# Cross attention and a routed FFN on one core: probabilities turned by transposing DMAs, attention products one body later

## What is computed

```python
q = x @ Wq + lora(x, q);  k = ctx[:, :73] @ Wk + lora(k);  v = ctx[:, :73] @ Wv + lora(v)
out = attention(q, k, v) + attention(q, ctx[:, 73:] @ Wk_ipa, ctx[:, 73:] @ Wv_ipa)
x = x + out @ Wo + bo + lora(out, o)              # x was normalised first
h = layernorm(x);  gate = h @ gate_w              # 8 experts, the best two with weights
x = x + sum over the two experts of  w * (act(h @ w1[e]) @ w2[e])
```

## Time and profile before

| | us |
|---|---|
| median of 3 runs (715.86 to 717.43) | 716.49 |
| the profiled execution | 715.26 |
| span of its profile | 713.5 |
| PE busy (90% of the span) | 639.0 |
| VectorE busy (73%) | 519.7 |
| POOL busy (68%) | 483.3 |
| ACT busy (63%) | 446.3 |

### The profile page before, as it was taken

One profiled execution on the slowest core, in us unless ns is written; L12 is line 12 of the kernel. 1 busy time (PEld: TensorE's weight loads), 2 busy tenths in 40 slices (PEclk: granted clock), 3 DMA queues, 4 the chain that ended last, 5 costly groups with the idle time before them and its releaser, 6 DMA issues. The chain is left out here.

```text
span 713.5 us, 22010 instructions
## 1 busy us (share of the span) xinstructions
PE 639.0 (90%) x7612; PEld 528.3 (74%) x7613; DVE 519.7 (73%) x1226; ACT 446.3 (63%) x768; POOL 483.3 (68%) x577
## 2 busy tenths in 40 slices
PE   6627799999999999999999999979999999999871
PEld 2215587788788888788788778757888888888751
DVE  3964679988988998898898898986577644445431
ACT  1436787778778778778778877854464454454330
POOL 3024645878878877977877887875677676556744
PEclk9999899999999999999999999999999999999997
DMA  8921111112111121111211211203769989655630
GB/s 263 322 79 21 32 34 52 48 45 68 47 55 57 47 62 50 59 53 48 75 36 48 80 32 48 78 16 77 119 124 136 133 119 139 92 82 87 86 48 6
DMA packets 87259, 55.31 MB, mean 78 GB/s; under 512 B 60784, under 2 KB 81520, under 8 KB 87216
## 3 DMA queue, kind: packets, MB, share of 16 engines
q1 hardware_dynamic: 73840, 37.41, 22.2%
q0 software_dynamic: 13376, 17.33, 13.4%
HBM read 20.27 MB, written 24.85 MB: 63 GB/s over the span
## 5 line engine op out<-in xcount | busy, mean ns | idle before, releaser
L527 POOL DMA_INDIRECT out_x<-pt_s,token_of x71 | 113.0, 1592 | 23.4 <-issue 21.4
L782 DVE TENSOR_TENSOR wq_s<-wk_s,wq_s 128x512 f16<-128x512 f32 (+1 forms) x78 | 51.5, 664 | 78.6 <-ACT wq_s L603 78.5
L598 ACT ACTIVATE wk_s<-ps 128x512 f32<-128x512 f32 (+1 forms) x78 | 43.5, 557 | 102.9 <-PE ps L1600 99.0
L1600 PE MATMUL ps<-ffnw,wq_s 128*128 x852 | 100.1, 273 | 6.3 <-DVE wq_s L782 4.8
L1600 PE MATMUL ps<-q_s,ffnw 128*128 128x256 f16 (+1 forms) x936 | 103.3, 264 | 2.1 <-issue 1.6
L959 POOL TENSOR_TENSOR prob<-prob,mx 128x1168 f32<-128x1168 f32 x64 | 77.6, 1233 | 37.6 <-DVE mx L1401 37.5
L1600 PEld LDWEIGHTS ps<-q_s,ffnw 128*128 x936 | 86.0, 98 | 15.2 <-issue 4.6
L1600 PEld LDWEIGHTS ps<-ffnw,wq_s 128*128 128x128 f16 x852 | 81.7, 98 | 19.8 <-issue 9.8
L1600 PE MATMUL ps<-wo_s,ot_s 128*128 128x256 f16 x768 | 89.4, 273 | 2.8 <-DVE ot_s L1338 2.8
L1600 PE MATMUL ps<-xt_s,wq_s 128*128 128x256 f16 x768 | 89.9, 279 | 1.9 <-DVE xt_s L1338 1.9
L1600 PEld LDWEIGHTS ps<-xt_s,wq_s 128*128 128x128 f16 x768 | 76.5, 100 | 13.0 <-issue 1.9
(11 more groups left out here) (232 smaller groups left out, 1176.0 us busy)
## 6 DMA issues: line engine op xcount, KB each, us to landing
wstage<-in_ffn_w SPq DMA_DIRECT2D x16, 512.0 KB, 3.6
x_sb<-in_x SPq DMA_DIRECT2D x4, 1024.0 KB, 10.8
out_x<-x_sb SPq DMA_DIRECT2D x16, 256.0 KB, 2.2
rows_dram<-wstage SPq DMA_DIRECT2D x8, 264.0 KB
out_x<-pt_s,token_of POOLq DMA_INDIRECT x71
pt_s<-in_wq SPq DMA_DIRECT2D x2, 512.0 KB, 4.4
pt_s<-in_wo SPq DMA_DIRECT2D x2, 512.0 KB, 8.4
rows_dram<-row_words,slot_i POOLq DMA_INDIRECT x64, 2.5
```

Of the source, the lines that this page charges most:

```text
L527: pool.indirect_dma_start(out_rows, bass.IndirectOffsetOnAxis(ap=token_of[:, j % UNROLL, c:c + 1], axis=0), y_sb[:, j % UNROLL, c, :], Non ...
L598: act.activation(h32[:, half, 0:2 * n], h_ps(t, j, half)[:, 0:2 * n], ACT.Silu, scale=1 / WSCALE).then_inc(silu_done, 1)
L782: dve.tensor_tensor(hs[:, j % 2, 1, 2 * half:2 * half + 2, 0:n], h32[:, half, 0:2 * n].rearrange("p (f n) -> p f n", f=2), hs[:, j % 2, 0, ...
L1600: last = pe.matmul(o, lhs(a, n), rhs(c, n), start=(i == 0), stop=(i == len(steps) - 1))
```

## The change

1. Scores of both token tiles stay in PSUM, in banks 0 to 2 and 3 to 5. ACT's copies are gone. VectorE takes the maxima from PSUM and subtracts them into `prob` (`shift`, now on VectorE, in four pieces each). Queries, keys and transposes of x use banks 0 to 3, so PE's `queries` wait for the shifts.
2. POOL's `shift` is gone. After `normalise`, ACT writes the high parts token-major into a new tile `p_hl` (`p_high`), POOL the low parts (`p_low`), and SP turns `p_hl` into `pt_s` by four transposing DMAs of 512 KB per body (`columns_p`). PE's transposes of probabilities and their copies remain in the last body alone. The sums are scaled by a new operation, 128x32.
3. Attention products of a body run in the next (`attend_all(b - 1)`); projection, norm, router and routing are one body later too, so three bodies are unrolled, and the last holds more.
4. x and the FFN weights share memory (`both`): weights of 12 to 15 wait until x of the first 8 batches has been stored. `place` lies in PSUM.

```diff
+        both = sb("both", [P, OWN * 2 * FW + TILES * DM * 2], F16)
+        p_hl = sb("p_hl", [P, TPB, 2, HEADS, P], F16)
-        place = sb("place", [P, TPB, EXPERTS], F32)
...
-            return ps[:, (6, 7, 4, 0)[k], :]
+        def queries_bank(b, k):
+            return ps[:, ((6, 7, 4, 0) if only(b, 0) else (0, 1, 2, 3))[k], :]
         def keys_bank(k, b):
+            return ps[:, ((5, 1) if only(b, 0) else (3, 0))[k], :]
+        def scores_bank(t, half, m):
             bank, n = scores_place(half, m)
+            return ps[:, 3 * t + bank, n * CTX:(n + 1) * CTX]
+        def x_bank(b):
+            return ps[:, 4 if only(b, 0) else 7 if only(b, 1) else 0, :]
...
+            def columns_p(t):
+                for part in (0, 1):
+                    sp.dma_start_transpose(pt_s[:, part, :, t * P:t * P + P],
+                                           p_hl[:, t, part].rearrange("p h n -> p (h n)")).then_inc(pt_in[t], 16)
...
                 if not first:
+                    load_fw(b + 1)
+                sp.wait_ge(p_lo, 2 * b + 1)
+                sp.wait_ge(v_mm, b + 1)
+                context_rest(ctx_v, b + 1, ctx_v_in)
+                columns_p(0)
+                if first:
+                    sp.wait_ge(p_lo, 2)
+                    load_fw(1)
+                else:
+                    sp.wait_ge(p_lo, 2 * b + 2)
+                    load_vipa(b)
+                columns_p(1)
...
-            def shift(b, t):
-                pool.wait_ge(mx_done, 2 * b + t + 1)
...
+            def p_low(b, t):
+                pool.wait_ge(p_hi, 2 * b + t + 1)
+                v = prob[:, t, :].rearrange("p (h j) -> p h j", j=CTX)
+                pool.tensor_tensor(p_hl[:, t, 1, :, 0:CTX], v, p_hl[:, t, 0, :, 0:CTX], ALU.subtract).then_inc(p_lo, 1)
...
-            def copy_scores(b, t):
...
+            def p_high(b, t):
+                act.wait_ge(p_ready, 2 * b + t + 1)
+                if not only(b, 0):
+                    act.wait_ge(pt_in[t], 32 * b)
+                act.activation(p_hl[:, t, 0, :, 0:CTX], prob[:, t, :].rearrange("p (h j) -> p h j", j=CTX), ACT.Copy
+                               ).then_inc(p_hi, 1)
...
-            def maxima(b, t):
-                dve.wait_ge(s_copied, 2 * b + t + 1)
+            def shift(b, t):
+                dve.wait_ge(s_mm, 2 * b + t + 1)
...
+                for sc, m, _ in pieces:
+                    for w, ks in ((0, slice(0, ORG)), (1, slice(ORG, CTX))):
+                        last = dve.tensor_reduce(m[:, w], sc[..., ks], AX, ALU.max)
                 last.then_inc(mx_done, 1)
+                dve.wait_ge(mx_done, 2 * b + t + 1)
+                if not only(b, 0):
+                    dve.wait_ge(p_lo, 2 * b + t - 1)
...
+                        last = dve.tensor_tensor(p[..., ks], part, m[:, w].unsqueeze(len(part.shape) - 1).to_broadcast(
+                            list(part.shape)), ALU.subtract)
+                last.then_inc(shifted, 1)
...
+                dve.tensor_scalar(sm[:, t], sm[:, t], 1 / PSCALE, None, ALU.mult).then_inc(sum_done, 1)
...
+            def attend_all(b):
+                for t in range(TPB):
+                    pe.wait_ge(pt_in[t], 32 * b + 32)
...
+                for k in range(4):
+                    if k == 2 and not only(b, 0):
+                        pe.wait_ge(x1_done, b)
+                    if k == 3 and not (isinstance(b, int) and b < 2):
+                        pe.wait_ge(slots, b)
+                    attend(b, k)
...
+                scores(b, 1)
...
+                if normed:
+                    project(b - 2, 1)
+                if routed:
+                    rank(b - 3)
+                pe.wait_ge(xt_split, b + 2)
+                pe.wait_ge(shifted, 2 * b + 1)
+                for k in range(3):
+                    queries(b + 1, k)
+                pe.wait_ge(shifted, 2 * b + 2)
+                queries(b + 1, 3)
+                if not first:
+                    attend_all(b - 1)
...
+                pe.wait_ge(q_split, 4 * b + 8)
+                if x_left:
+                    pe.wait_ge(xt_split, b + 3)
+                new_keys(b + 1)
+                if normed:
+                    pe.wait_ge(ot_split, 4 * b - 3)
+                    transpose_2(b - 2)
                 if not first:
                     project(b - 1, 0)
+                if normed:
+                    router(b - 2)
```

More of the change, by code:

```diff
@@ L288, in build @@
         acc_in = sem("acc_in")
+        acc_old = sem("acc_old")
+        p_hi = sem("p_hi")
+        p_lo = sem("p_lo")
+        pt_in = [sem(f"pt_in{t}") for t in range(TPB)]
         pad_in = sem("pad_in")
@@ L1054, in _ @@
             pool.wait_ge(misc_in, 32)
-            body(0)
-            body(1)
-            with pool.Fori(2, BATCH - 1) as b:
+            for b in range(3):
+                body(b)
+            with pool.Fori(3, BATCH - 1) as b:
                 body(b)
@@ L1499, in _, with body @@
             full_tiles, early_table, late_tables = tile_tables(dve)
[L1501 to L1502 removed]
+            def body(b, x_left):
+                first, normed = only(b, 0), not (isinstance(b, int) and b < 2)
+                routed = not (isinstance(b, int) and b < 3)
                 if routed:
[L1504 to L1522 removed]
+                    chain = pick_experts(b - 3)
+                shift(b, 0)
+                if first:
+                    xt(1)
+                shift(b, 1)
+                q(b + 1, 0)
+                q(b + 1, 1)
+                sums(b, 0)
+                if normed:
+                    attended(b - 2)
+                    statistics(b - 2)
+                if routed:
+                    place_rows(b - 3, chain)
+                q(b + 1, 2)
+                q(b + 1, 3)
+                sums(b, 1)
+                if not first:
+                    for k in range(4):
+                        ot(b - 1, k)
+                if x_left:
+                    xt(b + 2)
@@ L1842, in body @@
[L1842 to L1850 removed]
+                for k, free in ((5, 3), (6, 2), (7, 1)):
+                    pe.wait_ge(pt_split, free)
+                    transpose_probs(b, k)
@@ L1851, in body @@
                 pe.wait_ge(vipa_in, 16 * b + 16)
-                if first:
-                    pe.wait_ge(w_split_p, 3)
+                pe.wait_ge(pt_split, 8)
                 for k in range(4):
-                    pe.wait_ge(pt_split, 8 * b + 5 + k)
-                    if k == 1 and not first and not last:
-                        pe.wait_ge(slots, b)
-                        router(b - 1)
                     attend(b, k)
-            body(0, True, False)
-            body(1, False, False)
@@ L1863, in _ @@
-            with pe.Fori(2, BATCH - 1) as b:
-                body(b, False, False)
-            body(BATCH - 1, False, True)
+            for b in range(3):
+                body(b, True)
+            with pe.Fori(3, BATCH - 2) as b:
+                body(b, True)
+            body(BATCH - 2, False)
+            last_body(BATCH - 1)
             transpose_2(BATCH - 2)
```

470 lines of the change are left out of this document (239 added, 231 removed).

## The result

The changed kernel takes 752.46 us (median of 4 runs, 747.9 to 754.79) against 716.96 for the kernel before beside it: 1.0482 times as long, 95% interval 1.0438 to 1.0527. The forecast was 732, slower, with a range of 702 to 768. The side and the range held, but the loss is 35 us where 15 was forecast. The profiled execution after took 754.79 us, with a span of 753.0.

What follows compares the result with a forecast made beforehand. PE was busiest (25.25 of 26.19 us per body); afterwards VectorE and keys in series would bind at 26.2. 715.26 + 1.4 (head) + 11 x 0.0 - 3.2 (body 14) + 17 (tail) = 730.5, forecast 732 at the median; range 702 to 768.

Steps and rivals of the forecast that it cites:

- The path on VectorE: Loop body: VectorE's operations in program order from the end of the first scores to xt, 18.9 us.
- The scaling of the sums: New VectorE operation of 128x32, twice per body: 0.2 us each, up to 1.8 in the range beside POOL.
- PE's clock full in the loop: Sign expected in the profile after: PE's granted clock stays full (2.4 GHz) through the loop bodies.
- the likeliest case: Loop bodies bound by VectorE and keys in series, 26.2 us each; kernel slower, 722 to 741 us; chance 0.43.
- a rival of 0.12: PE's clock falls in the gap ahead of the keys: 1.5 to 3.4 us per body, 747 to 768; chance 0.12.
- the picks' stall: Head of VectorE's body: picks wait behind POOL's last low part, 0 to 1.65 us, taken as 0.6.
- the head: The three unrolled bodies 0 to 2: +1.4 us in all, range -3 to +6.
- the weights of the next body wait for the low parts; + 2: Body 0 in the head: the next body's FFN weights wait for the low parts; + 2 us.
- The transposing DMAs: SP issues four per body, taken as 2.5 us each; last lands 8.6 us into the next body, at no cost.
- the third rival: Transposing DMAs late: from 3.3 us per issue they hold the attention products; 750 to 775 us; chance 0.15.
- Body 14 and the tail: Body 14 gains 3.2 us; from last scores to first FFN product takes 52 against 34.8, +17 (8 to 22).
- the forecast's next link: Tail: heads of 15 stand behind the norm in ACT's queue, 4.5 us, ahead of VectorE's tables.

Runs made afterwards that it cites:

- The two runs that take the DMAs' wait away: Changed kernel with only the high halves turned by DMA, 744.94 us; changed kernel with all transposes kept but started earlier and body 0's weights loaded first, 742.71 us.
- the last run: Changed kernel with keys, transposes, load and tail changes together, plus eight idle products ahead of the attention products: 707.79 us, 0.9825 of the kernel before.
- both gaps filled: Changed kernel plus idle PE products, ten ahead of the keys and eight ahead of the attention products: 735.39 us, 1.0251 of the kernel before.
- the run with one gap filled: Changed kernel plus ten idle PE products ahead of the keys' wait for xt, bodies 2 to 14: 745.93 us, 1.0420 of the kernel before.
- the run with the load first: Changed kernel with body 0's load of FFN weights for body 1 issued ahead of the transposing DMAs: 745.26 us, 1.0415 of the kernel before.
- the run on the keys: Changed kernel with the keys' second half in bank 5, waiting for the heads' second low part, not xt: 741.18 us, 1.0345 of the kernel before.
- the run on the tail: Changed kernel with the norm of batch 14 ahead of the routing and scatters of 13 in the last body: 747.86 us, 1.0457 of the kernel before.

## Why the prediction was right and wrong

**Right: the mechanism.** The work taken from PE is gone and buys nothing, because the keys wait for xt at the end of VectorE's queue. The path on VectorE was put at 18.9 from the end of the scores and took 18.60 from the first maxima. The two runs that take the DMAs' wait away leave the body at 27.2, and the run that takes xt out of the keys' way has bodies of 24.0 among its eleven.

**Right: VectorE's terms.** The shift was put at 3.3 per token tile and takes 1.63 + 1.63; the low parts on POOL were put at 2.43 and take 2.45. The scaling of the sums was put at 0.2 with 1.8 as the end of its range: it takes 0.18 (POOL idle) and 0.31 to 0.44 in the loop, 1.27 in one body of it, and 1.23 and 1.33 in the last body, where POOL works beside it. That the range of this term comes back in the versions with a shorter body, up to 2.12 us, is what makes some of their bodies long (the last run).

```profile
488.06 1.23 DVE L1489 TENSOR_SCALAR sm<-sm 128x32 f32<-128x32 f32 x1
...
493.32 1.33 DVE L1489 TENSOR_SCALAR sm<-sm 128x32 f32<-128x32 f32 x1
```

The Trainium skill, page "SBUF — State Buffer", section "Who interferes with whom", lists this kind of operation among those that may contend with POOL; these rows, 0.18 against 1.33 for one shape, agree with it.

**Wrong: the body, by one choice.** The step that failed is "PE's clock full in the loop", with which the likeliest case was summed; the loss of the clock after the gap stood as a rival of 0.12, at 1.5 to 3.4 us per body and 747 to 768 us. That rival is what happened, at 1.83 per body or a little more, and its range holds the 752.46. The forecast had weighed one pair of rows, a wait of 3.37 with the clock at half and one of 3.40 with it full, as even evidence. But those two stand in the head, and the path itself said that the gap would come back in every body. What the runs showed in place of the choice: the mean granted clock was below 1.00 in all eleven loop bodies of the changed kernel (0.94 in ten, 0.88 in one), and with both gaps filled it stayed full and the body took 25.70. The length of a single wait does not decide alone. In the loop the clock fell after waits of 2.73 (the changed kernel), 2.79, 4.21 and 2.69 (three runs), and once after one of 1.98 (the last run); it did not fall after 1.73, 2.26 and 2.01, nor after 3.07 (the second line of the run with one gap filled) and 3.11 (ahead of the keys in body 3 of the run with the load first). So the even evidence was no misreading of the rows; the mistake was to sum with the clock full where a gap of about 3 us was forecast for every body. Against 26.2 the forecast's path was 0.5 too long, about the picks' stall of 0.6, which came in the first loop body alone (1.19): 26.2 - 0.5 + 1.83 = 27.53.

**Wrong: the head.** It was put at +1.4 and cost 6.7. The forecast's "the weights of the next body wait for the low parts; + 2" named the right wait and put it on body 0. The term left out what stands behind on ACT: its exponential of body 1 is queued after the split of these weights, and the load had to pass the first pair of transposes on SP too. The run with the load first takes 5.0 of body 1 back, and 4.4 of bodies 0 to 2.

**The transposing DMAs** were priced at 1.3 to 5 us of issue each, taken as 2.5, with 3.3 as the point from which they would hold the attention products. SP's timeline has 4.53 for the first pair of a body and 7.81 for the second, 3.1 each as a mean, and the table of DMAs 6.3 us to landing, where the forecast had 3.8:

```profile
342.13 4.53 SPq L904 DMA_TRANSPOSE pt_s<-p_hl  x2
...
320.31 7.81 SPq L904 DMA_TRANSPOSE pt_s<-p_hl  x2
...
pt_s<-p_hl SPq DMA_TRANSPOSE x60, 6.3
```

The last lands 11.9 us into the next body (330.67 less 318.77), where the forecast had 8.6, and PE is ready for it at 10.2. So PE did wait for them, by 1.73, as the third rival said, but at an issue under its 3.3: the landing took 2.5 longer than priced, and the first pair began 23.4 us into the body (342.13 less 318.77), where the forecast had 21. It cost the body little (27.53 with the wait, 27.19 and 27.23 in the two runs without it), because the keys' wait stood behind and took it up. A second wait in a row on one engine is not added to the first; it is found under it when the first is gone, as the run on the keys found it.

**Body 14 and the tail.** -2.3 for -3.2, and +20.2 for +17. The first links named were right: scatters of 13, then the norm of 14, as the run on the tail showed by taking 4.4 away. In the trace of the changed kernel PE waits for that norm:

```profile
521.86 1.11 PE L1865 MATMUL ps<-ident,x2n 128*128 128x128 f32 x4 [4.23 <-ACT x2n L1236]
```

From there the profile's chain goes on through PE's own products to the FFN, and not through the heads of 15, the forecast's next link: VectorE ends those at 524.80, and PE's products up to 525.93 stand ahead of their use. The size was met partly by luck. The forecast had no term for the 10.08 us in which PE waits for the DMAs of batch 14, so the router of 13 ended 28.2 us after the last scores in place of 22.7; the steps behind it took 26.8 in place of 29.3, which hid about half of that.

## What to carry to other kernels

When an order leaves the busiest engine a new gap in every turn of a loop, price the turn with PE's lower clock after the gap as the likeliest case, unless a row of the same kernel shows a gap of that place and length at the full clock. Before work is moved off an engine, follow which bank, and so which wait, gates the next piece of work there: here another bank for half of the keys, with an earlier start of the transposes, of one load and of one norm, turned 5% slower into 1.2% faster. When two waits lie near each other in length, expect that removing one shows the other. And when some bodies of one run are longer than others, compare a long one with a short one engine by engine before a cause is named: a scaling of 128x32, 0.18 us alone, made up the whole of a difference of 1.6 us.

## What the runs showed of the hardware

DMA transposes of 512 KB between two SBUF tiles held SP for 2.3 us each in the first pair of a loop body and for 3.9 each in the second, and landed after 6.3, against 1.26 and 3.8 for one of 256 KB out of DRAM: twice the bytes cost 1.8 to 3.1 times as long on the queue. A fall of the granted clock was short: in body 9 it was 0.50 from 341 to 343 and 1.00 from 344 on, and the mean price of these falls was 1.83 us per body or a little more. And a VectorE scaling of 128x32 that began 0.20 us behind a POOL product of 2.16 us took 2.00 us and ended 0.04 after it; beside an idle POOL it took 0.18.
